# Attention after a group norm on one core: quadrants of a column maximum exchanged by VectorE copies instead of a TensorE matmul

## What is computed

```python
def _L0_conv_ref(x, Wq, Wk, Wv, gamma):
    xf = x.reshape(B, C, H * W)                        # 4, 256, 4096
    f = jnp.einsum('qc,bcn->bqn', Wq, xf)              # 64 x 4096
    g = jnp.einsum('qc,bcn->bqn', Wk, xf)
    h = jnp.einsum('vc,bcn->bvn', Wv, xf)              # 256 x 4096
    scores = jnp.einsum('bqn,bqm->bnm', f, g)
    beta = jax.nn.softmax(scores, axis=1)              # over n
    o = jnp.einsum('bvn,bnm->bvm', h, beta)
    return (gamma[0] * o + xf).reshape(size)
x = x + _L0_conv_ref(_gn(x), Wq, Wk, Wv, gamma)        # _gn: 32 groups of 8 channels
```

## Time and profile before

| | |
|---|---|
| Median of 3 runs | 1927.73 us (1927.43 to 1928.16) |
| The profiled execution: time, span of the core | 1928.24 us, 1926.5 us |
| PE busy | 1888.7 us, 98% of the span |
| DVE busy | 1587.7 us, 82% |
| ACT busy | 1571.9 us, 82% |
| POOL busy | 1306.4 us, 68% |
| L505, the exchange on TensorE | 128 matmuls for 64 calls |
| Length of a chunk without extra work (first weight matmul to first weight matmul) | 27.42 us |
| Length of a chunk j = 12 or 15; j = 0 | 36.4 us; 39.2 us |
| Statistics in g = 3 of the chunks j = 1 to 4 (L991, two) | 1.24 us |

### The profile page before, as it was taken

The page is one execution under the profiler, slowest core; times in us unless marked ns, Lnnn a source line. Parts: engine busy times, 40 slices in busy tenths (PEclk is TensorE's granted clock), DMA queues, the critical chain, the costliest instruction groups (busy, mean ns, idle before and its releaser), DMA issues.

```text
span 1926.5 us, 44170 instructions
## 1 busy us (share of the span) xinstructions
PE 1888.7 (98%) x17476; PEld 1564.1 (81%) x17476; DVE 1587.7 (82%) x1932; ACT 1571.9 (82%) x1677; POOL 1306.4 (68%) x761
## 2 busy tenths in 40 slices
PE   5899999999999999999999999999999999999998
PEld 3678888877888888887888888888788888888887
DVE  7889898977778899987777889988777787888784
ACT  4788889977778888897877888898787788888885
POOL 4367678866656776886655776788575567766777
PEclk9999999999999999999999999999999999999999
DMA  4022112212112211211211211121130111111111
GB/s 139 8 67 72 51 32 74 56 23 64 32 36 59 74 54 26 75 53 32 60 36 40 78 45 54 53 55 45 28 78 18 23 31 32 34 23 32 32 34 34
DMA packets 199021, 91.18 MB, mean 47 GB/s; under 512 B 150176, under 2 KB 191392, under 8 KB 198816
## 3 DMA queue, kind: packets, MB, share of 16 engines
q1 hardware_dynamic: 198816, 88.36, 17.5%
HBM read 46.60 MB, written 16.78 MB: 33 GB/s over the span
## 4 chain that ended last, share of the span: by engine, by line
PE 93%; issue 0%; ACT 0%; DVE 0%; POOL 0%; DVEq 0%
PE O L496 23%; PE O L498 23%; PE O L497 23%; PE S L484 7%; PE S L481 7%; PE S L478 6%; PE O L455 1%; PE O L456 1%; PE O L457 1%; PE S L505 1%; PE O L440 1%; PE O L441 1%; PE O L445 1%; PE S L457 0%; PE S L456 0%
## 5 line engine op out<-in xcount | busy, mean ns | idle before, releaser
L381 POOL TENSOR_TENSOR PL<-SC,PH 128x1024 f16<-128x1024 f32 x511 | 1089.3, 2138 | 559.2 <-ACT SC L633 555.8
L496 PE MATMUL O<-V,PH 128*128 128x257 f16 x4096 | 1118.7, 273 | 0.5 <-POOL PL L409 0.4
L498 PE MATMUL O<-V,PL 128*128 128x257 f16 x4096 | 1118.5, 273 | 0.0
L497 PE MATMUL O<-V,PH 128*128 128x256 f16 x4096 | 1116.7, 273 | 0.0
L632 ACT ACTIVATE PH<-SC 128x1024 f16<-128x1024 f32 x511 | 539.1, 1055 | 119.0 <-PE O L498 110.8
L835 DVE TENSOR_TENSOR SC<-SC,MB 128x1024 f32<-128x1024 f32 x511 | 613.0, 1209 | 0.1
L626 ACT ACTIVATE SC<-S 128x1024 f32<-128x1024 f32 x512 | 502.8, 1013 | 115.4 <-issue 104.4
L795 DVE TENSOR_TENSOR XM<-S,XM 128x1024 f32<-128x1024 f32 x384 | 468.0, 1219 | 124.4 <-PE S L484 123.0
L633 ACT ACTIVATE SC<-SC 128x1024 f32<-128x1024 f32 x511 | 533.2, 1044 | 0.0
L496 PEld LDWEIGHTS O<-V,PH 128*128 128x128 f16 x4096 | 406.1, 99 | 49.4 <-POOL PL L409 0.9
L497 PEld LDWEIGHTS O<-V,PH 128*128 128x128 f16 x4096 | 400.9, 98 | 50.1
(11 more groups left out here) (106 smaller groups left out, 1064.3 us busy)
## 6 DMA issues: line engine op xcount, KB each, us to landing
xin<-x SPq DMA_DIRECT2D x24, 1024.0 KB, 5.7
xres<-x SPq DMA_DIRECT2D x64, 256.0 KB, 2.9
out<-RES SPq DMA_DIRECT2D x64, 256.0 KB, 2.2
ATT<-OT SPq DMA_DIRECT2D x1008, 16.0 KB, 1.9
F<-GG SPq DMA_DIRECT2D x64, 64.0 KB, 2.0
GG<-GG SPq DMA_DIRECT2D x32, 128.0 KB, 2.4
SC<-x SPq DMA_DIRECT2D x3, 1024.0 KB, 7.5
SC<-x SPq DMA_DIRECT2D x2, 512.0 KB, 10.7
```

The costliest lines, as they stand in the source:

```text
L381: pool.tensor_tensor(PL[:, s % RING, :], sc(s), PH[:, s % RING, :], ALU.subtract).then_inc(pl_ready, 1)
L496: mm(o[:, 0:C + 1], PH[:, n % RING, cols], vh, start=t == 0, stop=False)
L497: mm(o[:, 0:C], PH[:, n % RING, cols], vl, start=False, stop=False)
L498: w = mm(o[:, 0:C + 1], PL[:, n % RING, cols], vh, start=False, stop=t == T - 1)
```

## The change

The exchange between quadrants moves to VectorE. `quadrant_maxima` writes its reduce into SBUF (`mxq[:, 0, :]`) and then copies the 8 numbers a partition of quadrants 1, 2 and 3 into places 1 to 3 of quadrant 0, by three `tensor_copy` of 32 partitions x 8, SBUF to SBUF. `column_maxima` then reduces quadrant 0's 32 numbers a partition four times, each time writing `mxc` of another quadrant. The `share_maxima` matmuls, the multiply into `mxs`, the constants `place` and `alike` with the instructions that make them, and TensorE's wait for `mxc` go. In the start stage `maximum(G + 1)` moves behind the first half of the first subtraction, and ScalarE's `store(G + 1)` behind the first pair of exponentials.

```diff
@@ pool
-            pool.memset(alike[:, :], 0.0).then_inc(consts, 1)
-            for i, shift in enumerate(range(QP - P, P, QP)):
-                pool.wait_ge(consts, 4 + i)
-                pool.affine_select(out=alike[:, :], in_=alike[:, :], ...)
@@ tensor
-            def share_maxima(c, o):
-
-                pe.wait_ge(mxs_ready, c + 1)
-                mm(o[:, 0:NQ * NB], alike[:, :], mxs[:, :, :].rearrange("p i j -> p (i j)"),
-                   start=True, stop=True).then_inc(mx_shared, 1)
...
             scores(G)
             later_v(NV - 1)
-            share_maxima(0, shared0)
             scores(G + 2)
...
-                if g == 4 and 0 < k < K - 1:
-                    pe.wait_ge(mxc_ready, k + 2)
...
-                if n == 4:
-                    share_maxima(1, shared0)
-                if g == 3 and 0 < k < K - 1:
-                    read = min(n + 2 * G + 1, K * G)
-                    pe.wait_ge(s_stored, read)
-                    pe.wait_ge(s_maxed, read)
-                    share_maxima(k + 1, S[:, 0, :])
@@ scalar
-            store(G + 1)
             act.wait_ge(sub_first, 1)
             nc.scalar.activation(PH[:, 0, FIRST], sc(0)[:, FIRST], ACT.Exp, bias=SHIFT)
             nc.scalar.activation(sc(0)[:, FIRST], sc(0)[:, FIRST], ACT.Exp, bias=SHIFT).then_inc(exp_first, 1)
+            store(G + 1)
@@ vector
             def quadrant_maxima(c):
                 dve.wait_ge(mx_turned, c + 1)
-                ve.tensor_reduce(mxq, MT[:, :].rearrange("p (i j n) -> p j i n", i=GT, j=NB), axis=AX.XY,
-                                 op=ALU.max).then_inc(mxq_ready, 1)
+                if c > 0:
+                    dve.wait_ge(mxc_ready, c)
+                ve.tensor_reduce(mxq[:, 0, :], MT[:, :].rearrange("p (i j n) -> p j i n", i=GT, j=NB),
+                                 axis=AX.XY, op=ALU.max).then_inc(mxq_ready, 1)
                 dve.wait_ge(mxq_ready, c + 1)
-                if c == 0:
-                    dve.wait_ge(places, 2)
-                else:
-                    dve.wait_ge(mx_shared, c)
-                ve.tensor_tensor(mxs[:, :, :], place[:, :, :], mxq.unsqueeze(1).to_broadcast([P, NQ, NB]),
-                                 ALU.mult).then_inc(mxs_ready, 1)
-
-            def column_maxima(c, o):
-
-                dve.wait_ge(mx_shared, c + 1)
+                for i in range(1, NQ):
+                    r = ve.tensor_copy(mxq[0:QP, i, :], mxq[i * QP:(i + 1) * QP, 0, :])
+                r.then_inc(mxq_moved, 1)
+
+            def column_maxima(c):
+
+                dve.wait_ge(mxq_moved, c + 1)
                 if c > 0:
                     dve.wait_ge(mb_ready, c)
-                ve.tensor_reduce(mxc[:, :], o[:, 0:NQ * NB].rearrange("p (i j) -> p j i", i=NQ), axis=AX.X,
-                                 op=ALU.max).then_inc(mxc_ready, 1)
+                for q in range(NQ):
+                    r = ve.tensor_reduce(mxc[q * QP:(q + 1) * QP, :],
+                                         mxq[0:QP, :, :].rearrange("p i j -> p j i"), axis=AX.X, op=ALU.max)
+                r.then_inc(mxc_ready, 1)
...
             quadrant_maxima(0)
-            maximum(G + 1)
-            column_maxima(0, shared0)
+            column_maxima(0)
...
                                  ALU.subtract).then_inc(done, 1)
+                if part == FIRST:
+                    maximum(G + 1)
```

More of the change, by code:

```diff
@@ L33, in groupnorm_attention @@
     NB = M // QP
-    CONSTS = 3 + 1 + 2 * NQ - 1
+    CONSTS = 3
     EPS = 1e-5
@@ L108, in groupnorm_attention @@
         MT = sb("MT", [P, GW], f32)
-        mxs = sb("mxs", [P, NQ, NB], f32)
+        mxq = sb("mxq", [P, NQ, NB], f32)
         mxc = sb("mxc", [P, NB], f32)
-        place = sb("place", [P, NQ, NB], f32)
-        alike = sb("alike", [P, P], f32)
         rden = sb("rden", [P, MB2], f32)
@@ L132, in groupnorm_attention @@
         MB = ctx.enter_context(nc.psum_tensor("MB", [P, 512], f32))
-        mxq = MB[:, M:M + NB]
         gmean = MB[:, M + 32:M + 32 + NG]
@@ L137, in groupnorm_attention @@
         gd2 = MB[:, M + 128:M + 128 + 32].rearrange("p (a b) -> p a b", a=NG)
-        shared0 = MB[:, M + 192:M + 192 + NQ * NB]
         x0n = S[:, 0, :].rearrange("p (i n) -> p i n", i=2)
@@ L147, in groupnorm_attention @@
         consts = sem("consts")
-        places = sem("places")
         w_split = sem("w_split")
@@ L173, in groupnorm_attention @@
         mxq_ready = sem("mxq_ready")
-        mxs_ready = sem("mxs_ready")
-        mx_shared = sem("mx_shared")
+        mxq_moved = sem("mxq_moved")
         mxc_ready = sem("mxc_ready")
@@ L358, in _ @@
                                base=0, pattern=[[-1, P]], channel_multiplier=1).then_inc(consts, 1)
-            pool.memset(alike[:, :], 0.0).then_inc(consts, 1)
-            for i, shift in enumerate(range(QP - P, P, QP)):
-                pool.wait_ge(consts, 4 + i)
-                pool.affine_select(out=alike[:, :], in_=alike[:, :], compare_op=ALU.not_equal, fill=1.0,
-                                   base=shift, pattern=[[-1, P]], channel_multiplier=1).then_inc(consts, 1)
             pool.wait_ge(w_hi, 1)
@@ L883, in add_residual @@
                                  RES[:, k % 2, :, :], ALU.add).then_inc(last_ready, 1)
[L885 to L889, removed]
             ve.memset(cm[:, :], 0.0)
@@ L968, in _ @@
                 if n == 4:
-                    column_maxima(1, shared0)
+                    column_maxima(1)
                     spread_maxima(1)
@@ L980, in _ @@
                 if g == 3 and 0 < k < K - 1:
-                    column_maxima(k + 1, S[:, 0, :])
+                    column_maxima(k + 1)
                     spread_maxima(k + 1)
```

## The result

| | before | after |
|---|---|---|
| Median | 1927.43 us (1926.89 to 1928.16, 5 runs) | 2095.61 us (2094.72 to 2100.06, 5 runs) |
| The profiled execution: time, span | 1928.24 us, 1926.5 us | 2100.06 us, 2098.2 us |
| Granted TensorE clock, mean of the span | 0.999 | 0.969 |
| PE busy | 1888.7 us, 98% | 1938.6 us, 92% |

The ratio is 1.0874 [1.0862, 1.0886]: 8.7% slower, 168 us in the median. The profiled execution is the longest of the five, 4.5 us above the median. The forecast of 2050 had the sign and the mechanism; the time lies 10.6 us above the range's upper end of 2085. In the code after, the copies are L787, the maximum L769, the subtraction L811, the four reduces L796, the transpose to `MB` L804, the scores L468 to L474, the weights L486 to L488, the low weights L371.

What follows compares the result with a forecast made beforehand. TensorE, busy 399.84 of 400 us, was taken as the bound. 106.1 + 2.4 + 6.8 + 7.2 - 2.6 - 1.0 + 3.5 = +122.4 on 1928.24 gave 2050.6, about 2050 in the median; range 1938 to 2085.

Steps and rivals of the forecast that it cites:

- the waits of the copies: VectorE, g = 1: copies 1 and 2 each wait for a GpSimd low-weights instruction to end; g = 2's maximum starts 1643.35, not 1639.74.
- the stall: TensorE before the scores of g = 4 waits 2.30 us for VectorE's second maximum; chunk 2.04 longer net, 52 chunks: +106.1.
- the four reduces: VectorE, g = 3: four 32x32 to 32x8 reduces, each held until the last is done, take 0.87 us, net +0.65.
- The sum: All terms added: +122.4 us on the profiled execution's 1928.24, that is 2050.6; median about 2050.
- 6 with coefficients: Chunks with coefficients work in g = 3: 2.65 us against 1.0 left, taken as 1.1 over each, together 6.8.
- 12 with normalisation: Chunks with normalisation in g = 3: 2.2 us against 1.0 left, taken as 0.6 over each, together 7.2.
- 9 of j = 12, 15, 0: Chunks 9 to 12 us longer, GpSimd nearly over when copies come: -0.26 each; with chunk 62, 10 x -0.26 = -2.6.
- start and chunk 0: Start stage: store(G + 1) later, first weights +1.5 us (0 to 2); copies at chunk 0's end meet GpSimd, +2.0.
- By g = 0 VectorE has caught up, since g = 5 to 7 add nothing to it: VectorE after extra work in g = 3: lateness claimed gone by the next g = 0; no size given.
- Rival 2: Copies in g = 1 don't wait at all; maximum starts 0.48 later, within slack; -7.3 us, 1920; chance 0.15.
- Rival 1: Copies in g = 1 wait once, VectorE keeping the port; plain chunk net +0.13, total +21, 1949; chance 0.24.
- Rival 3: Copy 1 loses to GpSimd's second L381, later terms at upper values: 2070; copy 3 losing too, up to 2100; chance 0.09.

Runs made afterwards that it cites:

- e1_reduce: The changed kernel with its three copies written as tensor_reduce over an axis of length one; 1922.24 us, ratio 0.997 to the kernel before.
- e4_fill: The changed kernel with 20 unused f16 matmuls ahead of TensorE's wait for the maxima in g = 4, in 51 stalling chunks; 2064.87 us, ratio 1.0712.
- e8_cast: e4_fill with ScalarE's two casts of the normalised input cut to 128 of 1024 columns; 2067.33 us, ratio 1.0724.
- e10_both: e4_fill with both ScalarE's casts and VectorE's normalisations cut to 128 of 1024 columns; 2056.76 us, ratio 1.0671.
- e7_one_wait: The changed kernel with its first copy kept and the second and third written as reduces; 1964.03 us, ratio 1.0187.
- e5_start: e1_reduce with the start stage's maximum(G + 1) and store(G + 1) in the order of the kernel before; 1920.81 us, ratio 0.9962.
- e2_cross: The kernel before plus three dummy SBUF copies in g = 1, from quadrants 1 to 3 to quadrant 0; 2218.23 us, ratio 1.1507.
- e3_same: The kernel before plus three dummy SBUF copies in g = 1 that read and write quadrant 0 alone; 2137.21 us, ratio 1.1087.

## Why the prediction missed, point by point

**Right, within 0.05 us:** the waits of the copies and who makes them wait; the second copy losing to GpSimd's next instruction; the third passing; the stall (2.26 for 2.30); the four reduces (0.86 for 0.87), and with them that each is held until the one before is done; the plain chunk at full clock (29.42 for 29.46); the 52 chunks. The Trainium skill's rules cited in the prediction held here: in "SBUF — State Buffer", section "Who interferes with whom", a whole-instruction lock between GpSimd and the fast copies, and none for a reduce (e1_reduce, 0.148 to 0.153 us for all 192), and in "VectorE: DVE Perf Modes", section "Two Vector instructions with no wait between them", the hold between instructions of different quadrants (the four reduces, each begun 0.01 us after the end of the one before).

**The missing term: TensorE's clock.** "The sum" added 2.04 a chunk and nothing for what a stall does to the matmuls behind it. The kernel before gave no row with a stall of 2.3 in the steady part, and I put no bound in its place: a term taken as nothing without a reason. It is 31 us by e4_fill, where the same stall filled with matmuls keeps the clock at 0.997. Without it the time is 2065, inside the range. Why the clock falls behind some of these stalls and not behind others stays open.

**The classes.** The differences from before, in us, summed over the chunks of a kind (the profiled executions; that of the kernel after is the longest of its five, so its sum is 171.7 where the medians give 168.2); the second column is without the clock:

| | forecast | e4_fill | after |
|---|---|---|---|
| 22 plain chunks | 44.9 | 47.1 | 67.1 |
| 12 with statistics | 26.9 | 27.5 | 37.6 |
| 6 with coefficients | 19.0 | 17.9 | 21.2 |
| 12 with normalisation | 31.7 | 38.3 | 39.3 |
| 9 of j = 12, 15, 0 | -2.3 | 0.9 | 0.9 |
| the last two, L505's stalls | -1.3 | -0.1 | -0.1 |
| start and chunk 0 | 3.5 | 4.6 | 5.7 |
| sum | 122.4 | 136.2 | 171.7 |

**"By g = 0 VectorE has caught up, since g = 5 to 7 add nothing to it"** failed for normalisation: 6.6 more than forecast in e4_fill, and 2.2 more in the plain chunks, three of which stand behind such a chunk (j = 11) and are 1.0 longer than the others. I looked for the delay on VectorE alone. It goes round by ScalarE, full of casts or waiting for late subtractions, to the next chunk's first maximum (the rows of e4_fill, e8_cast and e10_both). The prediction did name that store of g = 2 as late, but followed it to TensorE's weights only.

**Long chunks and start.** Of the -0.26 forecast for j = 12 and 15 only -0.15 came (36.22 and 36.33 for 36.37 and 36.47), and in j = 0 TensorE now waits 0.8 us for its scores: +0.6 each instead. Chunk 0 cost 3.9 to 4.1, not 2.0; the first weights came 1.6 later in the kernel after and 0.7 in e4_fill (forecast 1.5). In the prediction's own sum, six times 1.1 for the coefficients is 6.6, not 6.8, which changes nothing.

**The rivals.** Rival 2's condition, that these copies don't wait, is false, but its price was right when e1_reduce made it true. Rival 1's term for the plain chunk was right (0.32 of stall for 0.39), its total 15 us low by the same terms as above, normalisation (6), the plain chunks (4) and the long ones (3), without any clock (e7_one_wait, 1964 for 1949). Rival 3 gave the place where the time fell, 2070 to 2100, by luck: its mechanism did not happen, no copy 1 lost to the second L381.

## What to carry to other kernels

A tiny VectorE copy between two SBUF tiles is not priced by its size but by where it falls in GpSimd's instructions: place each copy against them, and ask again for each next one; where it may fall inside one, write it as a reduce over an axis of length 1 (0.15 us, no wait). Before calling a lateness absorbed, follow it through every engine of the pipeline round to the next chunk, and for every new stall of TensorE of some 2 us give the clock behind it a term of its own. Before adding work in front of an instruction, look at the wait of that instruction itself: the old exchange had 0.1 us of slack where the scores behind it had 1.6.

## What was not expected of the hardware

- After a stall of 2.26 us TensorE's granted clock fell to the lower level for 3.4 us in 21 of 38 chunks, and in 17 it did not; chunks 53 and 56, one of each kind, have the same count of matmuls in the 12 us before. In the chunks 1 to 61 stalls of up to 1.7 us never did it (e1_reduce, e5_start, e7_one_wait); those of 3.6 us and more did in 52 of 52 (e2_cross), but of 3.3 to 4.4 us only 19 of 52 did (e3_same, clock 0.980). Chunk 60's stall of 2.25 us, alike in five kernels, left the clock alone in two and lowered it in three. So the length of the stall alone does not decide, and what does stays open.
- 20 matmuls of no use in the place of the stall keep the clock, and gained 30.7 us although the scores of a plain chunk start no earlier (14.32 us after its start, 14.31 without them).
- Of three copies queued without a wait, those that each read another quadrant pass one at a boundary of GpSimd's, those in one quadrant two.
- Making ScalarE's work 1.5 us shorter in the 12 chunks with normalisation made these chunks no shorter, but 2.0 us longer together (e8_cast against e4_fill). In them one VectorE instruction now falls behind a GpSimd one that it had preceded, and lasts 2.65 us instead of 0.80; that this is the whole reason is not shown.
